# An attention, expert-mixture and refinement layer on one core: four edits at the joints between its stages

## The reference

```python
# attention: 16 heads, 16 plain + 8 rotary features each, latent width 64
scores = einsum(Q, K); clip to +-80; causal; weights = softmax(scores / sqrt(24))
x1 = x + layernorm((weights @ V) @ W_O)            # Q, K, V from layernorm(x)

# mixture, on xn = layernorm(x1), v = 0 at first; two iterations
logits = gelu(xn @ router_w1 + b) @ router_w2 + b   # top 2 of 8 experts, from xn, once
for _ in range(2):
    ctx = [integrated, v]                           # 512 features
    a, b, g = gelu(ctx @ w1 + b1) @ w2 + b2         # one shared and two chosen experts: 3 x 256 outputs each
    v_next = sigmoid(a) * v - softplus(b) * (integrated - mu)
    x_next = integrated + 0.1 * sigmoid(g) * v_next
    # weighted over the three, then mixed in by a halting gate
# refinement and end
refined = gelu(integrated @ refine_w1 + b) @ refine_w2 + b
out = x1 + layernorm(xn + integration_weight * refined)
```

## Time and profile before

| | us |
|---|---|
| median of 3 runs | 2655.97 |
| lowest, highest | 2653.72, 2656.37 |
| the profiled execution | 2656.04 |
| its span, first to last instruction | 2654.3 |
| attention ends, mixture begins (by the trace) | about 999 |
| mixture ends, refine begins | about 2443 |

### The profile page before, as it was taken

One profiled execution on the slowest core, in us unless ns is written; L12 is line 12 of the kernel. 1 busy time (PEld: TensorE's weight loads), 2 busy tenths in 40 slices (PEclk: granted clock), 3 DMA queues, 4 the chain that ended last, 5 costly groups with the idle time before them and its releaser, 6 DMA issues. The chain is left out here.

```text
span 2654.3 us, 42371 instructions
## 1 busy us (share of the span) xinstructions
PE 2462.7 (93%) x15736; PEld 1751.5 (66%) x15736; DVE 2246.4 (85%) x3849; ACT 1888.9 (71%) x3011; POOL 635.3 (24%) x427
## 2 busy tenths in 40 slices
PE   5999999999999976999999999999999999999997
PEld 2333334333333335888888888888888888888997
DVE  5788887887887786989999999999999999977555
ACT  2787787878778845676767676766776777765886
POOL 2113221221322202112121211212121212110676
PEclk8999999999999977999999999999999999999999
DMA  6462644626264511000000000000010000003332
GB/s 134 76 100 85 104 90 80 110 73 100 84 104 76 124 41 43 10 26 10 17 26 26 11 17 26 26 10 19 24 26 11 21 21 18 18 1 102 117 120 80
DMA packets 149631, 146.50 MB, mean 55 GB/s; under 512 B 19922, under 2 KB 131794, under 8 KB 149428
## 3 DMA queue, kind: packets, MB, share of 16 engines
q1 hardware_dynamic: 149428, 143.80, 24.2%
HBM read 97.22 MB, written 46.53 MB: 54 GB/s over the span
## 5 line engine op out<-in xcount | busy, mean ns | idle before, releaser
L577 ACT ACTIVATE probs<-psum_a 128x1024 f32<-128x1024 f32 (+3 forms) x768 | 600.3, 815 | 201.7 <-PE psum_a L950 198.6
L1678 PE MATMUL psum_f<-w,picked 128*128 128x256 f32 (+1 forms) x2304 | 717.2, 344 | 0.0
L1677 PE MATMUL psum_f<-w,picked 128*128 128x256 f32 x2304 | 622.9, 287 | 12.2 <-DVE picked L1489 10.3
L1678 PEld LDWEIGHTS psum_f<-w,picked 128*128 128x128 f32 x2304 | 444.2, 193 | 51.4
L1677 PEld LDWEIGHTS psum_f<-w,picked 128*128 128x128 f32 x2304 | 444.2, 193 | 16.5 <-issue 11.9
L950 PE MATMUL psum_a<-q_stack,k_stack 72*128 72x512 f16 (+3 forms) x1536 | 380.7, 338 | 23.9 <-ACT probs L577 16.8
L660 DVE TENSOR_SCALAR probs<-probs 128x2048 f32<-128x2048 f32 (+3 forms) x320 | 320.1, 1000 | 83.0 <-ACT probs L577 82.8
L1489 DVE TENSOR_TENSOR picked<-hid,masks 128x512 fp32r<-128x512 f32 x512 | 369.7, 782 | 7.2 <-PE psum_f L1678 3.8
L1322 ACT ACTIVATE gates<-psum_f 128x256 f32<-128x256 f32 (+1 forms) x384 | 185.1, 487 | 249.8 <-PE psum_f L1678 208.6
L965 PE MATMUL psum_a<-probs,v 128*17 128x512 f32 (+3 forms) x3072 | 337.3, 512 | 11.8 <-DVE probs L660 5.0
L950 PEld LDWEIGHTS psum_a<-q_stack,k_stack 72*128 72x128 f16 x1536 | 98.9, 99 | 358.4 <-ACT probs L577 208.9
(11 more groups left out here) (299 smaller groups left out, 5168.5 us busy)
## 6 DMA issues: line engine op xcount, KB each, us to landing
heads_scratch<-kq_parts SPq DMA_DIRECT2D x64, 256.0 KB
k_stack<-heads_scratch SPq DMA_DIRECT2D x84, 128.0 KB
q_stack<-heads_scratch SPq DMA_DIRECT2D x84, 128.0 KB
x_in<-x_dram SPq DMA_DIRECT2D x8, 1024.0 KB, 5.5
x_res<-x_dram SPq DMA_DIRECT2D x16, 512.0 KB, 5.8
xs<-x_scratch SPq DMA_DIRECT2D x16, 512.0 KB, 3.9
xf_scratch<-xs SPq DMA_DIRECT2D x16, 512.0 KB, 2.9
xf<-xf_scratch SPq DMA_DIRECT2D x16, 512.0 KB, 6.2
```

Of the source, the lines that this page charges most:

```text
L577: act.activation(probs[:, s % PROB_SETS, 2 * u:2 * u + 2, q0:512], psum[:, 2 * u:2 * u + 2, q0:512], ACT.Exp, scale=exp_scale).then_inc(ex ...
L1677: pe.matmul(soft_out, x, cols[:, 1], start=start, stop=stop)
L1678: return pe.matmul(gate_out, x, cols[:, 2] if it == 0 else cols[:, 0::2], start=start, stop=stop)
```

## The change

Four edits.

1. **First stacks in three parts.** Sequence 0's stacks come as group 0, group 1, and groups 2 and 3, each part with its semaphore. That is 12 transfers more for each half; the bytes are the same.
2. **One bank in iteration 0.** b and g of a slot go into the slot's own bank by one product of 512 columns; softplus reads the first half of these banks.
3. **The seam into mixture.** For block 0, LG runs before EDGE, and MT after all of H. Block 1's RT, SHARED, EDGE, LG and H0 run before unit 0, H1 and H2 behind unit 0, MT behind unit 1 as before. POOL makes `x_scale(1)` first, then waits until block 0's `onehot` is ready, and only then makes the lower parts.
4. **The end of refine.** Row statistics are taken half by half, each behind its add. Blocks 14 and 15 are finished on DVE alone (`finish`: subtract and multiply for each of four tiles, then add x1), and not by DVE's shift, ACT's scaling and POOL's add.

```diff
 def load_first_stacks(half):
                 stack(0, 0, 1, cols, first_stacked[half][0])
-                stack(0, 1, GROUPS - 1, cols, first_stacked[half][1])
+                stack(0, 1, 1, cols, first_stacked[half][1])
+                stack(0, 2, GROUPS - 2, cols, first_stacked[half][2])
...
-                    pe.wait_ge(first_stacked[c][min(g, 1)], 16 * STACK_DMAS)
+                    pe.wait_ge(first_stacked[c][min(g, 2)], 16 * STACK_DMAS)
...
     def first_layer(k):
+        if k == 0:
+            return [[("RT", k, 0, 0), ("H", k, 0, SHARED), ("LG", k, 0, 0), ("H", k, 0, EDGE)],
+                    [("H", k, 0, 0), ("H", k, 0, 1), ("H", k, 0, 2)], [("MT", k, 0, 0)]]
...
         if kind == "first":
+            if gi == 0:
+                rows, h, _ = first_layer(k)
+                return [first_x(k) + rows + h[0:1], [("H", k, 0, 1), ("H", k, 0, 2)], [("MT", k, 0, 0)], []]
             return [first_x(k)] + first_layer(k)
...
             pool.wait_ge(weights_ready, 1)
+            x_scale(1)
+            pool.wait_ge(onehot_ready, 1)
             for m in (EDGE, *range(FULL)):
                 lower_parts(("H", 0, 0, m))
-            x_scale(1)
+            for job in fills(0)[0]:
+                if job in gel_turn:
+                    lower_parts(job)
...
-                src = soft_psum[:, slots.start * D:slots.stop * D]
+                if unit_of(n)[1] == 0:
+                    src = psum[:, AG_BANK + slots.start:AG_BANK + slots.stop, 0:D]
+                else:
+                    src = soft_psum[:, slots.start * D:slots.stop * D].rearrange("p (s n) -> p s n", n=D)
...
                 def both(x, w, start=False, stop=False):
+                    if it == 0:
+                        return pe.matmul(gate_out, x, w[:, D:3 * D], start=start, stop=stop)
...
+        DVE_LAST = 2
...
-                if k >= 3:
+                if 3 <= k < BLOCKS - DVE_LAST + 3:
                     pool.wait_ge(scaled, k - 2)
...
-                if k >= 2:
+                if 2 <= k < BLOCKS - DVE_LAST + 2:
                     scale(k - 2)
...
-                dve.wait_ge(dve_read, dve_value[("RF", k, 1)])
-                for t in range(BT):
-                    last = dve.bn_stats(stats[:, t, :], y[:, k % BUFS, t, :])
+                    dve.wait_ge(dve_read, dve_value[job])
+                    for t in (2 * i, 2 * i + 1):
+                        last = dve.bn_stats(stats[:, t, :], y[:, k % BUFS, t, :])
...
+            def finish(k):
+                dve.wait_ge(rstd_ready, k + 1)
+                rows = y[:, k % BUFS]
+                for t in range(BT):
+                    last = dve.tensor_scalar(rows[:, t, :], rows[:, t, :], y_mean[:, k % 2, t:t + 1], y_rstd[:, k % 2, t:t + 1],
+                                             ALU.subtract, ALU.mult)
+                then_wait(last)
+                dve.tensor_tensor(rows, rows, x1[:, k % BUFS], ALU.add).then_inc(y_last_ready, 1)
...
-            for k in range(-1, BLOCKS + 2):
+            for k in range(-1, BLOCKS + 1):
...
-                if k >= 2:
+                if 2 <= k < BLOCKS:
                     y_shifts(k - 2)
...
+            for k in range(BLOCKS - DVE_LAST, BLOCKS):
+                finish(k)
```

More of the change, by code:

```diff
@@ L308, in attention @@
         stacked = [sem(f"stacked{g}") for g in range(GROUPS)]
-        first_stacked = [[sem(f"first_stacked{half}{i}") for i in range(2)] for half in range(2)]
+        first_stacked = [[sem(f"first_stacked{half}{i}") for i in range(3)] for half in range(2)]
         scores_ready = sem("scores_ready")
@@ L355, in write_scratch @@
                 if b == 2:
-                    for i in range(2):
+                    for i in range(3):
                         sp.wait_ge(first_stacked[0][i], 16 * STACK_DMAS)
@@ L1329, in softplus @@
                     act.wait_ge(late.x1_stored, 16 * BLOCKS)
-                src = soft_psum[:, slots.start * D:slots.stop * D]
-                act.activation(soft_b[:, n % 2, slots], src.rearrange("p (s n) -> p s n", n=D), ACT.Softplus).then_inc(b_read, 1)
+                if unit_of(n)[1] == 0:
+                    src = psum[:, AG_BANK + slots.start:AG_BANK + slots.stop, 0:D]
+                else:
+                    src = soft_psum[:, slots.start * D:slots.stop * D].rearrange("p (s n) -> p s n", n=D)
+                act.activation(soft_b[:, n % 2, slots], src, ACT.Softplus).then_inc(b_read, 1)
             for item in order:
@@ L1786, in refine @@
         y_ready = sem("r_y_ready")
+        y_last_ready = sem("r_y_last_ready")
+        DVE_LAST = 2
         def bank(job):
@@ L1822, in _ @@
             for k in range(BLOCKS - 3, BLOCKS):
-                sp.wait_ge(y_ready, k + 1)
+                if k < BLOCKS - DVE_LAST:
+                    sp.wait_ge(y_ready, k + 1)
+                else:
+                    sp.wait_ge(y_last_ready, k - (BLOCKS - DVE_LAST) + 1)
                 sp.dma_start(out_v[k], y[:, k % BUFS]).then_inc(stored[k % BUFS], 16)
```

7 lines of the change are left out of this document (2 added, 5 removed).

## The result

The changed kernel takes 2644.05 us in the median of six runs (2641.48 to 2648.95), the kernel before 2657.07 beside it. The ratio is 0.9951, 95% interval 0.9941 to 0.9962: 13 us less, where 13.8 were predicted (the forecast of 2642.2 started from a median that was 1.1 lower). The profiled execution took 2643.47, with a span of 2641.6. The sum was right to a microsecond. Its terms were not: one was much too small and one much too large, and the misses made up for each other in part. That the sum came out so close is in good part luck.

What follows compares the result with a forecast made beforehand. PE and DVE bound the kernel by turns: DVE half of each mixture period, PE the other, waits at the seam, a DVE/POOL/ACT chain ending refine. 3.9 + 0.5 + 5.1 + 4.3 = 13.8 off 2656.04 gives 2642.2 us, range 2634 to 2648.5.

Steps and rivals of the forecast that it cites:

- in the upper bound only: First stacks: 5.9 us less if PE, at 1.2 GHz around the wait, keeps 2.4 GHz for lack of it.
- The next gap: Sign at the first stacks: PE's next gap after group 1's first scores stays below 1 us.
- The price of a pair: Mixture, iteration 0: one 512-column product for two of 256 saves 8.1 ns, 12.4 us of PE over 1536 pairs.
- (a): Seam: ACT reads LG at once, not behind EDGE's five, so route begins at about 1011.8 instead of 1013.96.
- (b): Seam: with POOL waiting for the table, route takes about 4.5 us; table ready at 1016.3, not 1021.5.
- (c): Seam: PE makes EDGE, H0 to H2, MT without waiting for route; MT 1017.8, masks' cast ends 1019.4, first pick 1030.5.
- (d): Seam: normalising block 1's x, beside up to three POOL operations, ends at 1024.5, against 1031.29 for XT before.
- (e): Seam: behind XT, 18 products, LG and H0; unit 0 begins at 1036.7, 3.8 later, but ends 0.8 us earlier.
- (f): Seam, unit 0 to end of group (0,0): DVE saves the 1.43 us LG wait and 2.9 us of POOL operations.
- A new wait behind unit 0: Sign at the seam: such a wait, or longer mixture periods, would show the forecast wrong.
- the seam gives nothing: Rival: five jobs ahead of unit 0 run at 1.2 GHz, picks wait for masks; 5.1 becomes 0, 2647.3 us; 10%.
- the exclusion: End of refine: by the skill page, POOL's root and block 14's four DVE multiplications take turns, so gain 3.6 us.

Runs made afterwards that it cites:

- once DVE has less to do: DVE leaves out two additions over the three slots in iteration 0: changed kernel so altered 2612.56 us, the same without edit 2 2626.69 us.
- With the clock kept up: Changed kernel plus 20 unread 512-column products on PE while it waits for block 1's normalised x: 2644.02 us, ratio 0.9949.
- two moves on DVE: Changed kernel with block 1's x normalised ahead of block 0's mask cast, and block 1's route before pick 2: 2637.71 us, ratio 0.9925.

## Why the prediction was right, and where it wasn't

**Edit 1: right place, too small.** Predicted 3.9, bounds 3.2 and 5.9; the runs show 6.8, above the upper bound. The mechanism held: group 1's stacks were there, nothing else came late. The failing step is the size. I took the gap of one trace, 3.87, for the price; over four traces the gap is 2.3 to 5.1, and behind it PE's products ran at 1.2 GHz. I had that in the upper bound only, with 2.0 us; it was 2.7 in the mean and there in all four (1.3 to 3.2). The next gap, 1.18 us, is a little above the 1 us I named, but it had stood there before.

**Edit 2: right for its reason, with a wrong price inside.** 0.5 predicted; no difference that the runs can tell. The price of a pair was too high: the four units of a group took 5.78 us in the mean and take 5.65, 0.13 / 24 = 5.3 ns a pair and 8 us in all, not 8.1 ns and 12.4. I had set the start intervals of first-layer products (232.4 ns) against those of a unit's pairs; inside a unit a 512-column product takes 5.65 / 24 = 235.5 ns. So picks waited 0.93 and not 1.4. The page "TensorE: Matmul & The Clock Gate" of the Trainium skill, section "Back-to-back issue gap", would have 2.5 ns, by the estimate from its formula for a lone product; the measurement lies between. None of it mattered for the sum, since the term was covered: edit 2 alone brings nothing that can be measured, and 0.39 us a period once DVE has less to do.

**Edit 3: wrong.** Predicted 5.1 less, bounds 1.5 and 9; it is 0.3 more in the profiled pair, about 1 more over all seven kernels, so below the lower bound. By its steps, with times from the seam's start in both kernels:
- (a) and (b) held: the route began at 12.3 (12.0 predicted) and had its table at 16.1 (16.5).
- (c) came late: EDGE to H2 ran in part at 1.2 GHz (24 products in 8.4 us), MT stood at 20.1 where I had 18.0, the cast ended at 21.4 where I had 19.6, and the picks stood at 32.3, predicted 30.7.
- (d) had the right length and the wrong start. From the cast's end to XT it took 5.1 us, as I had taken with POOL's three operations on the multiplications. But by (c) it began 1.8 late: XT at 26.5, predicted 24.7, bounds 22.2 and 25.5.
- (e) failed. Unit 0 began at 40.6 where I had 36.9, and its integration 3.1 us later than before, where I had 0.8 earlier. Of the 3.7 us, 1.8 came with XT from (c), 1.1 were the 18 products (7.0 us, where I took 5.9 between the two clocks), 0.8 LG and H0 behind them, at 1.2 GHz again. Before, one job stood ahead of unit 0; now six do, and they carry the clock that the wait for XT leaves. With the clock kept up the same 18 products took 4.4 us, and unit 0 began at 36.8. That this is my predicted 36.9 is chance: XT was as late there as in the changed kernel, and I had reckoned with half of the half clock.
- (f) held in part. I had summed 4.3 behind unit 0, 1.4 for the wait for LG and 2.9 for POOL's operations; from the integration to the group's end 41.3 became 38.5, 2.9 less (over the other kernels without edit 3 it is 40.5 to 41.3, so 2.0 to 2.9). The wait for LG went, and POOL held DVE by 2.0 us instead of 5.1 (the two additions over the slots in unit 0's integration took 3.38, not 1.42). But the new 1.73 us wait for the gates gave the 1.4 back. It stands in all seven kernels in which PE waits for block 1's table (1.7 to 2.3 us) and in none of the others. A new wait behind unit 0 is what I had named as a sign of being wrong.

The two steps close the account: unit 0 and its integration 3.9 us too late by (c) and (e), and 1.4 too little by (f), make 5.3 of the 5.4 between 5.1 less and 0.3 more. So the rival "the seam gives nothing" came true, at 10%, by one half of the mechanism that it named: the jobs ahead of unit 0 ran in good part at 1.2 GHz, but the masks were not late for it, since the picks stood at 32.3 and unit 0 at 40.6. What I had against it, that the same work had moved into waits of 6.4 us, is no argument when one of those waits is what lowers the clock.

**Edit 4: right.** 4.3 predicted, 4.8 measured, the upper bound. Of the 0.5, 0.3 is what I had set aside for the root holding DVE; the rest lies in the steps (7.5 us from the last product's end to DVE's, where I had 7.7). By the exclusion of "SBUF — State Buffer" of the Trainium skill, section "Who interferes with whom", my estimate had been 3.6. At the root the exclusion doesn't show: 1.37 us for four multiplications beside it. At the seam it does: the same four took 3.88 beside three POOL subtractions of 512 columns and 1.37 without them.

**The sum.** 6.8 + 0.8 - 1.1 + 4.8 makes 11.3, and the ratio gives 13 with 2.8 to either side. Against 3.9 + 0.5 + 5.1 + 4.3 = 13.8 the miss of edit 3, 6.2 too much, is half made up by edit 1, 2.9 too little, and edits 2 and 4, 0.8. The last 1.7 are within the interval; in the profiled pair the rest of mixture is 3.2 us shorter, with one fall of the clock fewer. So the mechanisms of edits 1, 2 and 4 were right, that of edit 3 was wrong, and that the sum still came out within 1 us is luck.

## What to carry to other kernels

Here a standstill of PE cost its length and the half clock behind it, and work that is moved ahead of a critical unit has to be priced at the clock that the standstill before it leaves. Before an order of jobs is changed, look for the waits of the engine that would do them: here two moves on DVE into waits of 4 and 7 us brought 7 us, and putting PE's jobs ahead of unit 0 brought none. A saving on the engine that is second by 0.6 us was worth nothing until the first was shortened, and then 0.39 us a period. A gap from one trace is one draw: compare the stretch over all the kernels that share it.
